# Reciprocal roots of the variances: ScalarE's logarithm and exp in place of VectorE's addition and GpSimd's power

## What is computed

```python
def _layernorm(x, axis=-1, eps=1e-05):
    m = jnp.mean(x, axis=axis, keepdims=True)
    v = jnp.var(x, axis=axis, keepdims=True)
    return (x - m) / jnp.sqrt(v + eps)
...
x = x + _L0_attn_ref(_layernorm(x, axis=-1), ...)
x = x + _L0_xattn_ref(_layernorm(x, axis=-1), ctx_1024, ...)
x = x + _L0_ffn_ref(_layernorm(x, axis=-1), ...)
# whose input is called y0, and which computes
y1 = _ln(y0 + _mha(y0, ...), ln1_g, ln1_b)
y2 = _ln(y1 + _moe(y1, ...), ln2_g, ln2_b)
```

## Time and profile before

| | before |
|---|---|
| device time, median of 3 runs | 422.02 us (417.72 to 423.76) |
| device time of the profiled execution | 419.1 us |
| its span, first to last instruction | 417.3 us |
| mean granted clock of TensorE | 0.949 |
| TensorE busy | 360.8 us, 86% of the span |
| VectorE busy | 286.2 us, 69% |
| ScalarE busy | 167.0 us, 40% |
| GpSimd busy | 119.7 us, 29% |

### The profile page before, as it was taken

One profiled execution on the slowest core, in us unless ns is written; L12 is line 12 of the kernel. 1 busy time (PEld: TensorE's weight loads), 2 busy tenths in 40 slices (PEclk: granted clock), 3 DMA queues, 4 the chain that ended last, 5 costly groups with the idle time before them and its releaser, 6 DMA issues.

```text
span 417.3 us, 10727 instructions
## 1 busy us (share of the span) xinstructions
PE 360.8 (86%) x4057; PEld 233.2 (56%) x4057; DVE 286.2 (69%) x742; ACT 167.0 (40%) x462; POOL 119.7 (29%) x153
## 2 busy tenths in 40 slices
PE   2687888988999789999999999884989979789994
PEld 1334455555665454646455555562545535679994
DVE  4844686566656777777887875445777749638996
ACT  2133353445565353535455453341768842200000
POOL 1126352000012335452212211039534423401111
PEclk9978998999999999999999999995999999659999
DMA  8998415144321111010000000000000000000001
GB/s 238 313 278 227 137 34 143 42 129 120 118 64 49 43 28 52 27 52 2 2 0 5 0 3 2 1 2 0 2 1 2 0 2 2 2 0 2 27 27 50
DMA packets 23283, 23.22 MB, mean 56 GB/s; under 512 B 3657, under 2 KB 18905, under 8 KB 23105
## 3 DMA queue, kind: packets, MB, share of 16 engines
q1 hardware_dynamic: 20944, 18.93, 15.7%
q0 software_dynamic: 1280, 3.15, 2.5%
q10 hardware_dynamic: 1008, 0.46, 0.4%
HBM read 15.91 MB, written 6.62 MB: 54 GB/s over the span
## 4 chain that ended last, share of the span: by engine, by line
PE 76%; DVE 8%; issue 7%; ACT 6%; DMA 1%; another core or an unknown queue 1%; POOL 1%; ACTq 0%; POOLq 0%; DVEq 0%
PE ps L991 8%; PE ps L1031 8%; PE ps L1045 7%; PE ps L1284 7%; PE ps L987 4%; PE ps L1025 3%; PE ps L1001 3%; PE ps L947 3%; PE ps L1075 3%; PE ps L1109 3%; PE ps L960 3%; PE ps L1182 2%; PE ps L1122 2%; PE ps L1274 2%; PE ps L1230 2%
## 5 line engine op out<-in xcount | busy, mean ns | idle before, releaser
L770 ACT ACTIVATE pT<-ps 128x512 f32<-128x512 f32 x128 | 75.1, 616 | 109.8 <-PE ps L1001 104.5
L374 DVE TENSOR_REDUCE m_pad<-ps 128x8 f32<-128x1024 f32 x32 | 39.2, 1224 | 44.6 <-PE ps L1031 39.9
L653 POOL TENSOR_TENSOR rstd<-veps,minus_half 128x1 f32<-128x1 f32 x32 | 19.0, 593 | 153.0 <-DVE veps L339 153.0
L350 DVE TENSOR_TENSOR p_sb<-qk_sb,heads 128x512 f32<-128x512 f32 x64 | 44.0, 687 | 0.8 <-ACT qk_sb L783 0.4
L377 DVE TENSOR_REDUCE m_pad<-ps 128x8 f32<-128x1024 f32 x32 | 38.9, 1215 | 0.0
L1031 PE MATMUL ps<-p_sb,qk_sb 32*128 32x512 f32 x256 | 38.9, 668 | 0.0
L991 PE MATMUL ps<-p_sb,qk_sb 32*128 32x512 f32 x256 | 38.6, 651 | 0.0
L1045 PE MATMUL ps<-pT,p_sb 128*32 128x128 f32 x1024 | 35.8, 282 | 2.3 <-ACT pT L770 2.3
L1284 PE MATMUL ps<-mexp,pT 128*128 128x128 f32 x256 | 33.8, 288 | 0.6 <-DVE pT L627 0.6
L1001 PE MATMUL ps<-mT,negsel 32*128 32x128 f32 x512 | 33.2, 357 | 1.2 <-issue 1.2
L1284 PEld LDWEIGHTS ps<-mexp,pT 128*128 128x128 f32 x256 | 31.5, 201 | 0.8 <-DVE pT L627 0.8
(11 more groups left out here) (178 smaller groups left out, 734.5 us busy)
## 6 DMA issues: line engine op xcount, KB each, us to landing
wkv_sb<-wkv SPq DMA_DIRECT2D x23, 128.0 KB
kv_sorted<-room SPq DMA_DIRECT2D x5, 512.0 KB, 4.8
ctx_sorted<-room SPq DMA_DIRECT2D x1, 1472.0 KB, 12.3
tk<-fside SPq DMA_DIRECT2D x1, 1024.0 KB, 9.6
out<-y SPq DMA_DIRECT2D x8, 128.0 KB, 1.8
x_sb<-x SPq DMA_DIRECT2D x1, 768.0 KB, 7.9
kv_sorted<-room SPq DMA_DIRECT2D x1, 384.0 KB, 4.4
causal<-c_causal ACTq DMA_DIRECT2D x1, 256.0 KB, 5.0
```

Source lines behind the costliest of these rows:

```text
L350: return dve.tensor_tensor(dst, rows.unsqueeze(1).broadcast_to([128, QUADS, S]), heads[:, 0, :].unsqueeze(2).broadcast_to([128, QUADS, S]) ...
L374: dve.tensor_reduce(m4[:, 0:2, 0:QUADS], ps[:, 0:2, :].rearrange("p g (j k) -> p g j k", j=QUADS), AX.X, ALU.max).then_inc(s["max_low"], 1)
L653: pool.tensor_tensor(rstd[:, :], veps[:, :], minus_half[:, :], ALU.pow)\
L770: act.activation(pT[:, t % 2, g, :, :], quad[4 + g], ACT.Exp).then_inc(s["exped"], 1)
```

## The change

VectorE's additions and GpSimd's powers go. ScalarE computes the logarithm of the variance with EPS as a bias from a column (`eps_col`), and then the exp of -0.5 times that. `norm_root(p+4)` and `y0_root(p-21)` stand behind the fourth exp of a period (in the periods before 0, `norm_root` stands first). `y0_root` runs one period later than `y0_power` did, in the same period in which VectorE uses it. In the y1 stretch a pair's root stands ahead of the copies of y1T of the pair before it. For the last norm the eight pairs stand at the end of ScalarE's program. The diff, cut:

```diff
-            dve.memset(minus_half[:, :], -0.5).then_inc(s["ones_ready"], 1)
-            dve.memset(half16[:, :], -0.5).then_inc(s["ones_ready"], 1)
+            dve.memset(eps_col[:, :], EPS).then_inc(s["ones_ready"], 1)
...
-            def norm_variance(t):
-                dve.wait_ge(s["bn_step"], 2 * t + 2)
-                if t >= 1:
-                    dve.wait_ge(s["pow_done"], t)
-                dve.tensor_scalar(veps[:, :], mv[:, 1:2], EPS, None, ALU.add).then_inc(s["veps_ready"], 1)
-
             def norm_rows(t):
-                dve.wait_ge(s["pow_done"], t + 1)
+                dve.wait_ge(s["root_done"], t + 1)
                 if t >= 1:
...
-            def y0_variance(b):
+            def y0_aggregate(b):
                 dve.wait_ge(s["st_step"], b + 1)
                 dve.bn_aggr(mv16[:, b, :], st16[:, b, :]).then_inc(s["mv_step"], 1)
-                dve.wait_ge(s["mv_step"], b + 1)
-                dve.tensor_scalar(ve16[:, b:b + 1], mv16[:, b:b + 1, 1], EPS, None, ALU.add)\
-                    .then_inc(s["ve_ready"], 1)
 
...
                     norm_aggregate(3)
-                    norm_variance(3)
                     bucket_slots()
                     norm_rows(3)
...
-            def pair_variance(b, k):
+            def pair_aggregate(b, k):
 
                 dve.wait_ge(s["st_step"], B * (k + 1) + b + 1)
                 for a in (b - 1, b):
                     dve.bn_aggr(mv16[:, a, :], st16[:, a, :]).then_inc(s["mv_step"], 1)
-                dve.wait_ge(s["mv_step"], B * (k + 1) + b + 1)
-                dve.tensor_scalar(ve16[:, b - 1:b + 1], mv16[:, b - 1:b + 1, 1], EPS, None, ALU.add)\
-                    .then_inc(s["ve_ready"], 1)
...
-            def norm_power(t):
-                pool.wait_ge(s["veps_ready"], t + 1)
-                if t >= 1:
-                    pool.wait_ge(s["xn_ready"], t)
-                pool.tensor_tensor(rstd[:, :], veps[:, :], minus_half[:, :], ALU.pow)\
-                    .then_inc(s["pow_done"], 1)
...
-            def y0_power(b):
-                pool.wait_ge(s["ve_ready"], b + 1)
-                pool.tensor_tensor(rs16[:, b:b + 1], ve16[:, b:b + 1], half16[:, b:b + 1], ALU.pow)\
-                    .then_inc(s["rs_ready"], 1)
-
             for p in PERIODS:
-                if live(p + 4):
-                    norm_power(p + 4)
-                if 0 <= p - Y0_STATS < B:
-                    y0_power(p - Y0_STATS)
...
-            def powers(k):
-
-                for i in range(B // 2):
-                    pool.wait_ge(s["ve_ready"], B + k * (B // 2) + i + 1)
-                    pool.tensor_tensor(rs16[:, 2 * i:2 * i + 2], ve16[:, 2 * i:2 * i + 2], half16[:, 0:2], ALU.pow)\
-                        .then_inc(s["rs_ready"], 1)
-
-            powers(0)
...
+            def norm_root(t):
+
+                if t == 0:
+                    act.wait_ge(s["ones_ready"], 1)
+                act.wait_ge(s["bn_step"], 2 * t + 2)
+                act.activation(lnvar[:, :], mv[:, 1:2], ACT.Ln, bias=eps_col[:, :]).then_inc(s["ln_step"], 1)
+                act.wait_ge(s["ln_step"], t + 1)
+                if t >= 1:
+                    act.wait_ge(s["xn_ready"], t)
+                act.activation(rstd[:, :], lnvar[:, :], ACT.Exp, scale=-0.5).then_inc(s["root_done"], 1)
+
+            def y0_root(b):
+                act.wait_ge(s["mv_step"], b + 1)
+                act.activation(lnvar16[:, b:b + 1], mv16[:, b:b + 1, 1], ACT.Ln, bias=eps_col[:, :])\
+                   .then_inc(s["ln16_step"], 1)
+                act.wait_ge(s["ln16_step"], b + 1)
+                act.activation(rs16[:, b:b + 1], lnvar16[:, b:b + 1], ACT.Exp, scale=-0.5).then_inc(s["rs_ready"], 1)
+
+            def pair_roots(k, i):
+                n = B + k * (B // 2) + i + 1
+                act.wait_ge(s["mv_step"], B * (k + 1) + 2 * i + 2)
+                act.activation(lnvar16[:, 2 * i:2 * i + 2], mv16[:, 2 * i:2 * i + 2, 1], ACT.Ln, bias=eps_col[:, :])\
+                   .then_inc(s["ln16_step"], 1)
+                act.wait_ge(s["ln16_step"], n)
+                act.activation(rs16[:, 2 * i:2 * i + 2], lnvar16[:, 2 * i:2 * i + 2], ACT.Exp, scale=-0.5)\
+                   .then_inc(s["rs_ready"], 1)
...
             for p in PERIODS:
+                if p < 0 and live(p + 4):
+                    norm_root(p + 4)
                 if live(p):
...
                     exp_group(p, 3)
+                if p >= 0 and live(p + 4):
+                    norm_root(p + 4)
+                if 0 <= p - Y0_STATS - 1 < B:
+                    y0_root(p - Y0_STATS - 1)
                 if live(p - 1):
                     copy_heads(p - 1)
                 if live(p + 3) and p != -1:
...
+            pair_roots(0, 0)
             for b in range(B):
+                if b % 2 == 0 and b + 2 < B:
+                    pair_roots(0, b // 2 + 1)
                 act.wait_ge(s["y1T_done"], b + 1)
                 act.copy(y1T[:, b, :], bank[4 + b % 2][:, 0:128]).then_inc(s["y1T_copied"], 1)
                 if b in (1, 9):
...
             act.copy(keptT_bf[:, :], bank[4][:, 0:128]).then_inc(s["keptT_copied"], 1)
             act.copy(keptT[:, :], bank[4][:, 0:128]).then_inc(s["keptT_copied"], 1)
+            for i in range(B // 2):
+                pair_roots(1, i)
```

More of the change, by code:

```diff
@@ L104, in decoder_kernel @@
         mv = sb("mv", [128, 2])
-        veps = sb("veps", [128, 1])
-        minus_half = sb("minus_half", [128, 1])
+        lnvar = sb("lnvar", [128, 1])
+        eps_col = sb("eps_col", [128, 1])
         rstd = sb("rstd", [128, 1])
@@ L161, in decoder_kernel @@
         mv16 = sb("mv16", [128, B, 2])
-        ve16 = sb("ve16", [128, B])
-        half16 = sb("half16", [128, B])
+        lnvar16 = sb("lnvar16", [128, B])
         rs16 = sb("rs16", [128, B])
@@ L199, in decoder_kernel @@
             kvs_odd_stored kv_in_0 kv_in_1 kv_in_2 kv_in_3 kv_in_4 kv_in_5 kv_in_6 kv_in_7 times_in x_in x_more_in x_rest_in wqkv_in attn_w_in ctx_in xw_in
-            ffn_w_in ones_ready wq_ready w_ffq_ready bn_step veps_ready pow_done xn_ready xT_done xnT_copied
+            ffn_w_in ones_ready wq_ready w_ffq_ready bn_step ln_step root_done xn_ready xT_done xnT_copied
             qkv_done qk_copied v_copied v_placed kTm_ready qTm_ready s_low s_high max_low max_high mT_done
@@ L204, in decoder_kernel @@
             stored m_done m_copied cb_done b1w2_ready crep_done
-            crep_copied st_step mv_step ve_ready rs_ready y0_ready y0_biased f_xT_done f_xT_copied
+            crep_copied st_step mv_step ln16_step rs_ready y0_ready y0_biased f_xT_done f_xT_copied
             qk_done qT_ready kblk_zeroed k_ready k_last_ready v_done v_ready f_s_done f_least_ready f_exped
@@ L302, in _ @@
             pairs = vaug.rearrange("p u h c -> p (u h c)").rearrange("p (m c) -> p m c", c=64)
-            dve.wait_ge(s["ones_ready"], 5)
+            dve.wait_ge(s["ones_ready"], 4)
             dve.memset(pairs[:, :, 8:9], 1.0).then_inc(s["ones_ready"], 1)
@@ L489, in _ @@
                     norm_aggregate(p + 4)
-                    norm_variance(p + 4)
                 if p == -4:
@@ L511, in _ @@
                 if 0 <= p - Y0_STATS < B:
-                    y0_variance(p - Y0_STATS)
+                    y0_aggregate(p - Y0_STATS)
                 if 0 <= p - Y0_ROWS < B:
@@ L591, in _ @@
                 if b < B and b % 2:
-                    pair_variance(b, 0)
+                    pair_aggregate(b, 0)
             routed = [0]
@@ L642, in _ @@
                 if 0 <= b < B and b % 2:
-                    pair_variance(b, 1)
+                    pair_aggregate(b, 1)
         @block.gpsimd
         def _(pool):
-            pool.wait_ge(s["ones_ready"], 2)
-            def norm_power(t):
-                pool.wait_ge(s["veps_ready"], t + 1)
-                if t >= 1:
-                    pool.wait_ge(s["xn_ready"], t)
-                pool.tensor_tensor(rstd[:, :], veps[:, :], minus_half[:, :], ALU.pow)\
-                    .then_inc(s["pow_done"], 1)
             def scatter_ctx(b):
@@ L740, in _ @@
                                    .then_inc(s["cblk_ready"], 1)
-            powers(1)
         @block.scalar
@@ L787, in place_v @@
                 if t == 0:
-                    act.wait_ge(s["ones_ready"], 7)
+                    act.wait_ge(s["ones_ready"], 6)
                 if t >= 4:
@@ L997, in less_max @@
                 if t == 0:
-                    pe.wait_ge(s["ones_ready"], 8)
+                    pe.wait_ge(s["ones_ready"], 7)
                 for j in range(QUADS):
@@ L1081, in count_buckets @@
                 pe.wait_ge(s["sort_in"], 48)
-                pe.wait_ge(s["ones_ready"], 3)
+                pe.wait_ge(s["ones_ready"], 2)
                 hots = hotT.rearrange("p b e -> p (b e)")
```

## The result

The changed kernel takes **557.24 us** (median of 4 runs, 554.7 to 560.01) against 420.38 in the same session (4 runs, 417.72 to 423.76): ratio 1.325, 95% interval 1.312 to 1.339. I forecast 530, with a range of 503 to 568.

The account below looks back on a forecast made before the run. TensorE was taken to bound the kernel (76% of the chain), ScalarE having 0.8 us of slack a period. Root terms of 99.9 plus 10.5 for the clock made a span of 527.7, with 1.8 outside it 530 us; range 503 to 568.

Parts of the forecast that it names:

- the forecast's own range: Whole kernel: 504 to 553 us, from a root of 2.8 to 3.4 us and a clock loss of 0 to 17.
- rival 3: TensorE falls to 1.2 GHz in one-root periods too, 1.5 us in some 21 periods: +31, 561 us; chance 0.13.
- rival 4: Half of a table load is hidden, a root costs 2.5 us: 32 us less, 498 us; chance 0.10.
- R = 3.1: Price in us of one root on ScalarE: two table loads of 1.28, logarithm 0.26, exp 0.15, four handoffs of some 0.03.
- Rival 1: Each table switch costs twice a load, a root 5.5 us: 127 us more, 657 us; chance 0.09.
- The slack of 0.8 us: ScalarE's part of a loop period is 6.21 us, TensorE needs 7.02; the change can spend only the 0.8 between.
- The clock term: Periods 21 to 27: key scores after TensorE's idle gap may run at half clock, 1.5 us seven times, +10.5.
- My last sign of being wrong: Whole kernel: the prediction is wrong if TensorE's clock falls everywhere; it expected below 1.00 in periods 21 to 27.
- The start: Before the loop: roots of tiles 1, 3 and 2 delay copies and first maxima by 5.2, 3.1 and 0.6: +8.9 us.
- Periods 12 to 15: Four local loop periods with one root each: 35.5 us against 30.05, +5.5.
- The y1 stretch: Behind the loop: first root, then seven roots and copies in one ScalarE queue, 371.95 against 361.95: +10.0 us.
- Rival 2: One table serves both functions, no load in the loop, a root costs 0.5 us: about 421 us, not slower; chance 0.03.

Follow-up runs that it names:

- e2: e1 with one needless load of the same table set ahead of each logarithm, half the changed kernel's loads; 484.01 us, ratio 1.150.
- e1: The changed kernel with one table set for logarithm and exp loaded by name at the start, all other loads gone; 428.24 us, ratio 1.017.
- e10: As e4, with 32 unread matmuls in place of 48 per one-root period and 92 in place of 96 with two; 540.04 us, ratio 1.279.
- e4: The changed kernel with unread matmuls filling TensorE's gap, 48 per one-root period, 96 with two; 540.35 us, ratio 1.284.
- e9: The changed kernel, both loads per root, with GpSimd waiting for a variance ahead of each period's scatters; median 544.3 us, ratio 1.293.
- e5: e1 with GpSimd waiting for a variance ahead of each period's scatters; 421.64 us, ratio 1.001 against the kernel before.
- e8: The kernel before, powers still on GpSimd, with each scatter behind a semaphore of its own; 417.16 us, ratio 0.988.

## Why the prediction was right

**The sum and the range.** My parts came to 110.4 us and the span grew by 140.9. The measured 557 is above the forecast's own range, 504 to 553; it is inside 503 to 568 only because I had added half of rival 3 at the top. That this was enough is in part luck: a third of the missing 30.5 us, 10.2, is a stop at the start that no rival of mine described. The lower end, 503, doesn't follow from my working either: half of rival 4 below 504 is 488.

**R = 3.1.** Right: 3.12. The logarithm took 0.29 (0.26 forecast), the exp 0.20 (0.15), the handoffs 0.01 to 0.02. Rival 1 (a drain with each switch) and rival 4 (half a load hidden) fall with this row and with e2. The Trainium skill's drain of about 1380 ns with every switch (ScalarE: Activation LUTs, "What ACT_TABLE_LOAD costs") doesn't show in any run here: the measurement decides. Where ScalarE is idle the first load runs ahead of the wait, as said.

**The slack of 0.8 us.** Right. A root of 0.46 us leaves the period at 7.0 (e1), one of 1.73 makes it 7.8 to 7.9 and one of 3.12 makes it 9.1 to 9.2 at the full clock (e2, e10, periods 19 and 20); forecast 9.31 for the last. With two roots 12.43 against 12.58.

**The clock term.** The mechanism was right and the size too small: 10.5 us against some 17 (e4, e10). The two-root periods lost 1.8 us each, not 1.5. Those with one root, which I gave nothing, ran at 0.90 in periods 16 to 20 and lost about 0.7: (51.31 - 48.02) / 5, e4's sum behind the minus. Against the 9.1 to 9.2 us of e10's periods 19 and 20, which no gather lengthens, it is 1.1. Rival 3 was true in its condition, not in its price: in place of its +31 the clock took some 6.5 beyond my 10.5. My last sign of being wrong, a clock that falls everywhere, came true as well: it fell in every group of periods. And I had misread a row: the 3.57 us of the earlier trace rows are ScalarE's wait for TensorE, not TensorE's own. TensorE's wait there is 3.36 us, from 285.07 to 288.43, and the clock had fallen before it, while TensorE was busy 0.86 of 2 us, in short pieces:

```profile
282.00:284.00 2.00, 0.86 (x3) 0.36 (x2) 1.82 (x8) 0.27 (x1) 1.73 (x3) 0.65 0.00 0
284.00:286.00 2.00, 0.62 (x2) 0.18 (x1) 1.54 (x3) 0.53 (x2) 1.75 (x2) 0.50 0.00 0
```

**The start: the step that failed.** I wrote 8.9 us, and that the scatters "have time to spare either way". The 8.9 was near: 7.7 to the copy of the first maxima, and with the scatters held (e9) 9.2 to the first exp. The scatters had time to spare themselves, but ScalarE didn't: the start cost 19.1. The term that was missing is the stop behind back-to-back scatters; 6.6 us of it reach the end by e1 and e5, some 13 by e9. The sign was in the trace of before: first exps of tiles 0 and 6 lie 47.97 us apart, and the timeline between them has two waits with no releaser named, 5.28 and 2.58 us, each behind a burst of scatters. I read past them.

**Periods 12 to 15** (+11.2 against 5.5) ran at a clock of 0.84. At the full clock (e10) they still took 39.1 us and not 35.5, and there the first exps of tiles 13 to 16 start 4.1 us in all behind TensorE's last matmul, just behind a gather each. In the changed kernel that is 0.3 us in all: its matmuls end later beside the same gathers. My sum had neither term.

**The y1 stretch** (+12.0 against 10.0): cblk, which before had run while VectorE was idle, now met its last rows, 3.2 us. That leaves 8.8 for the roots; a pair takes 3.44 us (477.91 to 481.35, copy to copy), where I had said 3.8. I had not asked what GpSimd would do beside a shifted VectorE.

**Rival 2** described the kernel that was not built. Its 421 came out as 428 (e1), and 421.64 once the scatters were paced (e5). The set exists, as the Trainium skill says (ScalarE: Activation LUTs, "Table sets: the hidden batching unit"); but the loads had been placed function by function, each from its own set, and only asking for the shared one removed them.

## What to carry to other kernels

When a function that is new to ScalarE goes into a loop with exp, look for one table set that serves both and load it by name first; otherwise count each load at 1.28 us and set it against the slack of ScalarE's cycle, not against its idle share. When work is taken off an engine, ask what else its time had been spacing: here a power's wait for its variance held DMA bursts back. And when a slow step is moved behind one waiter, list every engine that waits for it, with what is queued behind each, or the wait only changes its place.

## What the hardware showed

- A table load takes 1.283 us also when the same set is loaded again, and the instruction behind it starts 0.01 to 0.02 us later (e2, 64 loads).
- Indirect DMAs on GpSimd can hold up ScalarE's next instruction. In the changed kernel and in e1 the exp came 2.4 us after the last of 16 back to back (43.13 + 0.97 to 46.46; in e1 40.15 + 0.97 to 43.52), 9.85 and 11.25 us behind the matmul that it needed. Behind the burst of 4 of the kernel before it came 0.5 us after the last (33.63 + 1.43 to 35.56), and behind gathers 0.50 to 0.74 us. With a semaphore ahead of each scatter no such unnamed wait was left (e8).
- Not every instruction beside such a DMA is held: in the changed kernel ScalarE still ran up to 29.52 while the train had begun at 23.63, and in e9 it went on from 39.02 to 42.55 beside four scatters. By what path they hold it stays open. In the start the 16 DMA engines are also busy with loads (a DMA share of 1.04 from 24 to 36 us in the changed kernel); whether the long stop needs that too was not tried.
- TensorE's granted clock fell in periods in which it waited 2.2 to 2.3 us of some 10 for ScalarE's copy, to 0.90 on average, and to 0.81 where it waited 5.2 to 5.4 of 14. With the gaps filled it was 1.00 (e4).
